# Edge sums of a graph attention kernel: score parts accumulated on TensorE, a logit as a maximum of two sums, and the clamp at zero behind the exponential

## What is computed

```python
def gnn_ref(xn, src, dst, W, att_src, att_dst):
    xp = xn @ W                          # layer 1: by head, 8 x 32
    a_src, a_dst = xp @ att_src, xp @ att_dst
    e = leaky_relu(a_src[src] + a_dst[dst], 0.2)
    emax = segment_max(e, dst)           # a bound serves as well
    ex = exp(e - emax[dst])
    denom = segment_sum(ex, dst)
    return segment_sum(ex[:, None] * xp[src], dst) / denom
```

## Time and profile before

| | |
|---|---|
| runs | 1872.51, 1877.23, 1879.56 us; median 1877.23 |
| the profiled execution's own time | 1874.21 us, span 1872.5 us |
| PE, busy share of the span | 1518.0 us, 81% |
| DVE | 1154.5 us, 62% |
| ACT | 658.4 us, 35% |
| POOL | 1009.8 us, 54% |
| mean granted TensorE clock | 0.924 |

### The profile page before, as it was taken

The page is one execution under the profiler, slowest core; times in us unless marked ns, Lnnn a source line. Parts: engine busy times, 40 slices in busy tenths (PEclk is TensorE's granted clock), DMA queues, the critical chain, the costliest instruction groups (busy, mean ns, idle before and its releaser), DMA issues. The chain is left out here.

```text
span 1872.5 us, 33346 instructions
## 1 busy us (share of the span) xinstructions
PE 1518.0 (81%) x9468; PEld 1261.2 (67%) x9468; DVE 1154.5 (62%) x3311; ACT 658.4 (35%) x2160; POOL 1009.8 (54%) x1093
## 2 busy tenths in 40 slices
PE   5488888898898968999845887878888867899990
PEld 4355656687775657999823776766666656799990
DVE  7586767775686662222174988878888888412214
ACT  4432222234334653333234334533233236432320
POOL 3577776777771003555404777777777721255540
PEclk9699999899999989999968999999999985999995
DMA  6533333344340056676563444444444304677657
GB/s 143 145 106 106 107 104 83 106 107 108 106 107 25 1 190 199 208 214 211 151 164 95 108 110 109 109 109 109 109 109 109 107 5 138 187 214 213 212 165 208
DMA packets 147994, 244.17 MB, mean 130 GB/s; under 512 B 53370, under 2 KB 83369, under 8 KB 147559
## 3 DMA queue, kind: packets, MB, share of 16 engines
q0 software_dynamic: 48384, 134.19, 26.0%
q1 hardware_dynamic: 97306, 106.27, 19.4%
q10 hardware_dynamic: 2124, 1.54, 0.4%
HBM read 210.48 MB, written 31.21 MB: 129 GB/s over the span
## 5 line engine op out<-in xcount | busy, mean ns | idle before, releaser
L683 POOL DMA_INDIRECT es_rows<-table,eall x784 | 746.1, 952 | 336.6 <-issue 235.0
L703 PE MATMUL bank<-es_msg,es_one 128*125 128x264 f32 x976 | 255.1, 406 | 88.9 <-DVE es_msg L826 88.8
L703 PE MATMUL bank<-es_rows,es_won 128*125 x976 | 262.5, 415 | 70.2 <-DVE es_won L823 69.7
L766 ACT ACTIVATE es_oneT<-bank 125x512 bf16<-125x512 f32 x244 | 145.3, 596 | 365.2 <-PE bank L722 364.8
L703 PEld LDWEIGHTS bank<-es_msg,es_one 128*125 128x125 f32 x976 | 177.2, 191 | 126.1 <-DVE es_msg L826 98.3
L703 PEld LDWEIGHTS bank<-es_rows,es_won 128*125 128x125 f32 x976 | 185.6, 200 | 104.2 <-issue 76.6
L1400 DVE TENSOR_TENSOR xT<-bank,xT 128x256 f32<-128x256 f32 x112 | 47.5, 424 | 327.1 <-PE bank L1251 327.1
L1294 ACT ACTIVATE xT<-bank,ffn_b1s 128x128 f32<-128x128 f32 x448 | 128.1, 369 | 299.9 <-PE bank L1241 299.9
L1241 PE MATMUL bank<-ffn_xbT,ffn_w 128*128 128x128 f32 x1792 | 219.6, 276 | 0.0
L1251 PE MATMUL bank<-ffn_w,xT 128*128 x896 | 211.6, 379 | 0.0
L1241 PEld LDWEIGHTS bank<-ffn_xbT,ffn_w 128*128 128x128 f32 x1792 | 210.4, 193 | 0.1
(11 more groups left out here) (447 smaller groups left out, 2338.7 us busy)
## 6 DMA issues: line engine op xcount, KB each, us to landing
ffn_w<-in_L_ffn_W SPq DMA_DIRECT2D x112, 512.0 KB
es_rows<-table,eall POOLq DMA_INDIRECT x784
ffn_w<-yrows SPq DMA_DIRECT2D x20, 560.0 KB
ffn_w<-in_L_ffn_W SPq DMA_DIRECT2D x2, 4096.0 KB
xrows<-acc SPq DMA_DIRECT2D x10, 560.0 KB
table<-acc SPq DMA_DIRECT2D x5, 577.5 KB
table<-acc SPq DMA_DIRECT2D x5, 564.4 KB
out_x<-xs SPq DMA_DIRECT2D x5, 560.0 KB
```

What stands on the lines that cost most here:

```text
L683: pool.indirect_dma_start(rows[:, q % R, w, :], None, m.table[H], bass.IndirectOffsetOnAxis(ap=m.eall[:, at:at + 1], axis=0)).then_inc(gat ...
L703: ins = pe.matmul(sum_banks[p % 2][0:P, 0:W], left, right, start=(w == 0), stop=(w == BW - 1))
L766: a.activation(oneT[:, p % 2, :], turn_bank[0:P, :], ACT.Copy).then_inc(kept, 1)
```

## The change

It moves work from the edge to the node and from DVE to PE, and reorders DVE's queue. The maximum is written as `max(s + (a - m), 0.2 s + (0.2 a - m))`. The two values `a - m` and `0.2 a - m` are prepared per node, ahead of the loop, with two more operations. The three bf16 parts are no longer side by side but are added by PE in PSUM: twelve score matmuls of 2H columns instead of four of 6H. The reduce and the buffer `near` go. Two operations read the scores from PSUM, and a third takes the maximum. The clamp goes from the z group: the weighing takes `min(weight, 1)` within its one instruction (it becomes a scalar_tensor_tensor), and with eight heads ACT makes the second exponential from a Relu. The wait for `ready` and two of the z group's operations now stand ahead of the mark. The scores of step p wait for these two of step p - 1.

```diff
                 def scores(p):
                     pe.wait_ge(kept, p + 1)
                     if p >= 1:
-                        pe.wait_ge(zchain, 4 * p - 3)
+                        pe.wait_ge(branched, 2 * p)
                     for w in range(BW):
-                        ins = pe.matmul(scores_of[p % 2][:, w, :], oneT[:, p % 2, w * 128:(w + 1) * 128],
-                                        stage[:, p % 4, :], start=True, stop=True)
+                        for c in range(3):
+                            ins = pe.matmul(scores_of[p % 2][:, w, :], oneT[:, p % 2, w * 128:(w + 1) * 128],
+                                            stage[:, p % 4, c * 2 * H:(c + 1) * 2 * H], start=(c == 0), stop=(c == 2))
                     ins.then_inc(scored, 1)
...
                         a.activation(wts[:, p % 2, :, :], z[:, p % 2, :, :], ACT.Exp).then_inc(exped, 1)
+                        a.activation(below[:, p % 2, :, :], z[:, p % 2, :, :], ACT.Relu, scale=-1.0).then_inc(bounded, 1)
                         if p >= 2:
                             a.wait_ge(summed, p - 1)
-                        a.activation(msg[:, p % 2, :, D:D + H], z[:, p % 2, :, :], ACT.Exp).then_inc(laid, 1)
+                        a.wait_ge(bounded, p + 1)
+                        a.activation(msg[:, p % 2, :, D:D + H], below[:, p % 2, :, :], ACT.Exp, scale=-1.0).then_inc(laid, 1)
...
-                k.link(v.tensor_copy(piece[0], whole))
-                k.link(v.tensor_tensor(rest[:, :, :], whole, piece[0], ALU.subtract))
+                k.link(v.tensor_tensor(whole[:, :, 0:H], reach, top, ALU.subtract))
+                k.link(v.scalar_tensor_tensor(whole[:, :, H:2 * H], reach, SLOPE, top, ALU.mult, ALU.subtract))
+                k.link(v.tensor_copy(piece[0], whole[:, :, :]))
+                k.link(v.tensor_tensor(rest[:, :, :], whole[:, :, :], piece[0], ALU.subtract))
...
-                        v.tensor_tensor(won[:, p % 2, :, :], one[:, p % O, :, :], wts[:, p % 2, :, :].to_broadcast([128, BW, P]),
-                                        ALU.mult).then_inc(weighed, 1)
+                        v.scalar_tensor_tensor(won[:, p % 2, :, :], wts[:, p % 2, :, :].to_broadcast([128, BW, P]), 1.0,
+                                               one[:, p % O, :, :], ALU.min, ALU.mult).then_inc(weighed, 1)
...
                     if valid(p3):
+                        here = rows_of(p3, D, D + H)
+                        v.wait_ge(ready, p3 + 1)
                         v.wait_ge(scored, p3 + 1)
-                        v.tensor_reduce(near[:, p3 % 2, :, :], scores_of[p3 % 2].rearrange("p w (c x) -> p w x c", c=3),
-                                        AX.X, ALU.add).then_inc(zchain, 1)
+                        if H > 1 and p3 >= 2:
+                            v.wait_ge(laid, p3 - 1)
+                        v.tensor_tensor(zq, here, scores_of[p3 % 2][:, :, 0:H], ALU.add).then_inc(branched, 1)
+                        v.scalar_tensor_tensor(yq, here, SLOPE, scores_of[p3 % 2][:, :, H:2 * H], ALU.mult, ALU.add).then_inc(branched, 1)
                     if valid(p):
                         mark(p)
                     if valid(p3):
-                        here = rows_of(p3, D, D + H)
-                        v.wait_ge(ready, p3 + 1)
-                        v.wait_ge(zchain, 4 * p3 + 1)
-                        if H > 1 and p3 >= 2:
-                            v.wait_ge(laid, p3 - 1)
-                        v.tensor_tensor(zq, here, near[:, p3 % 2, :, 0:H], ALU.add).then_inc(zchain, 1)
-                        v.wait_ge(zchain, 4 * p3 + 2)
-                        v.scalar_tensor_tensor(yq, zq, SLOPE, zq, ALU.mult, ALU.max).then_inc(zchain, 1)
-                        v.wait_ge(zchain, 4 * p3 + 3)
-                        v.tensor_tensor(zq, yq, near[:, p3 % 2, :, H:2 * H], ALU.subtract).then_inc(zchain, 1)
-                        v.wait_ge(zchain, 4 * p3 + 4)
-                        v.tensor_scalar(zq, zq, 0.0, None, ALU.min).then_inc(zed, 1)
+                        v.wait_ge(branched, 2 * p3 + 2)
+                        v.tensor_tensor(zq, zq, yq, ALU.max).then_inc(zed, 1)
```

More of the change, by code:

```diff
@@ L613, in edge_sums @@
         stage = sb("_stage", [P, 4, 3 * 2 * H], BF16)
-        near = sb("_near", [128, 2, BW, 2 * H])
         if H == 1:
@@ L621, in edge_sums @@
         early = (won if H == 1 else msg)[0:P, :, :, :].rearrange("p a w x -> p (a w x)")
-        rest = early[:, 0:NT * 2 * H].rearrange("p (t x) -> p t x", t=NT)
+        rest, whole = [early[:, i * NT * 2 * H:(i + 1) * NT * 2 * H].rearrange("p (t x) -> p t x", t=NT) for i in range(2)]
         z = sb("_z", [128, 2, BW, H])
         y = sb("_y", [128, 2, BW, H])
+        below = sb("_below", [128, 2, BW, H])
         gathered = [sem(f"_gathered{r}") for r in range(R)]
-        landed, freed, split, split_chain, marked, turned, kept, scored, zchain, zed, exped, weighed, summed, added = [
-            sem(n) for n in ("_landed", "_freed", "_split", "_split_chain", "_marked", "_turned", "_kept", "_scored", "_zchain", "_zed",
-                             "_exped", "_weighed", "_summed", "_added")]
+        landed, freed, split, split_chain, marked, turned, kept, scored, branched, zed, exped, bounded, weighed, summed, added = [
+            sem(n) for n in ("_landed", "_freed", "_split", "_split_chain", "_marked", "_turned", "_kept", "_scored", "_branched", "_zed",
+                             "_exped", "_bounded", "_weighed", "_summed", "_added")]
         ends_set, laid, ready = sem("_ends_set"), sem("_laid"), sem("_ready")
@@ L640, in edge_sums @@
         wts = m.bank[6][:, NBLK * BW:NBLK * BW + 2 * BW * H].rearrange("p (s w h) -> p s w h", s=2, w=BW)
-        scores_of = [m.bank[1][:, i * BW * 6 * H:(i + 1) * BW * 6 * H].rearrange("p (w x) -> p w x", w=BW) for i in (0, 1)]
+        scores_of = [m.bank[1][:, i * BW * 2 * H:(i + 1) * BW * 2 * H].rearrange("p (w x) -> p w x", w=BW) for i in (0, 1)]
         def valid(p):
@@ L788, in _ @@
                     v.tensor_tensor(self_z[:, :, :], self_z[:, :, :], m.adm[:, :, 1:2], ALU.subtract).then_inc(self_zed, 1)
-                whole = m.adm[:, :, 0:2 * H]
+                reach, top = m.adm[:, :, 0:H], m.adm[:, :, H:2 * H]
                 piece = [parts[:, :, i * 2 * H:(i + 1) * 2 * H] for i in range(3)]
@@ L822, in weigh @@
                             v.wait_ge(summed, p - 1)
-                        v.tensor_tensor(won[:, p % 2, :, :], one[:, p % O, :, :], wts[:, p % 2, :, :].to_broadcast([128, BW, P]),
-                                        ALU.mult).then_inc(weighed, 1)
-                    else:
-                        v.tensor_tensor(msg[:, p % 2, :, 0:D].rearrange("p w (h x) -> p w h x", h=H),
-                                        rows_of(p, 0, D).rearrange("p w (h x) -> p w h x", h=H),
-                                        wts[:, p % 2, :, :].unsqueeze(3).to_broadcast([128, BW, H, D // H]),
-                                        ALU.mult).then_inc(weighed, 1)
+                        v.scalar_tensor_tensor(won[:, p % 2, :, :], wts[:, p % 2, :, :].to_broadcast([128, BW, P]), 1.0,
+                                               one[:, p % O, :, :], ALU.min, ALU.mult).then_inc(weighed, 1)
+                    else:
+                        v.scalar_tensor_tensor(msg[:, p % 2, :, 0:D].rearrange("p w (h x) -> p w h x", h=H),
+                                               wts[:, p % 2, :, :].unsqueeze(3).to_broadcast([128, BW, H, D // H]), 1.0,
+                                               rows_of(p, 0, D).rearrange("p w (h x) -> p w h x", h=H),
+                                               ALU.min, ALU.mult).then_inc(weighed, 1)
                 for i in range(STEPS + 5):
```

## The result

The changed kernel takes **1889.14 us** (median of 20 runs, 1881.63 to 1902.51); the kernel before took 1874.44 in the 20 runs beside them (1867.54 to 1880.32). The ratio is 1.0085, with a 95% interval of 1.007 to 1.010: 0.85% slower, 14.7 us. The forecast was 1898 us: +20.7 on the 1877.23 us that the first three runs of the kernel before gave. The profiled execution took 1892.33 us with a span of 1890.5, 18.0 us more than the span before, so the trace shown is of a run somewhat above the median.

The account below looks back on a forecast made before the run. The prediction saw the first stage paced by PE and its handover with DVE, with gathers near as the next limit. Terms of +19.2 us (first stage) and +1.5 (second) gave +20.7 on 1877.23: 1898 us, range 1864 to 1928.

Parts of the forecast that it names:

- Scores on PE: Eight more score matmuls add 0.20 us per iteration on PE's path: +13.2 us first stage, +4.8 second.
- The z group behind a wait: DVE's steps after waiting for ready: z to add grows to 1.00 us, costing +8.4 us first stage, +2.9 second.
- Without a wait: First-stage iterations where DVE is never idle: reduce to add falls from 1.45 to 1.00 us, 13 times, -5.9 us.
- The new wait of PE: PE's next scores wait for both sums, which wait for ready; late every eighth iteration, 15 x 0.2 = +3.0 us.
- Weighing and ScalarE: The weighing's new form with the clamp, and ScalarE's Relu plus second Exp in the second stage, cost nothing.
- A weighing at half rate: Rival: the weighing's new form runs at half rate, mainly in the second stage; about 1950 us, chance 0.04.
- Second stage outside the pairs: Second-stage steps before about 1290 us and after 1500: DVE's savings bring 1.4 us just before the pairs, 4.8 together after.
- the pair: Two iterations of the second stage's loop through PE and DVE, predicted at about 9.07 us instead of 8.75.
- The ring's waits of POOL: Gathers' waits for a free slot among eight blocks, 14.8 us before, predicted to grow by some 15 us.
- DVE sets the pace: Rival: DVE's total work limits both stages, so six operations instead of eight make it faster; 1850 us, chance 0.15.
- the matmuls fall into PE's waits: Rival: the added score matmuls hide in PE's waits for the weighing, leaving +2.7 us; 1880 us, chance 0.15.
- Adding in place: Rival: score matmuls adding into the same columns stall PE at 182 ns each; +113, 2011 us, chance 0.04.

Follow-up runs that it names:

- experiment 8: The changed kernel with the mark ahead of the wait for ready and its twelve score matmuls issued twice (24): 1895.78 us, ratio 1.0119.
- experiment 1: The kernel before, with each score matmul issued three times into the same place, nothing else changed: 1891.43 us, ratio 1.009.
- experiment 3: The changed kernel with the mark put back ahead of the wait for ready, twelve score matmuls kept: 1860.46 us, ratio 0.9917.
- experiment 4: The changed kernel with mark ahead of the wait for ready, four wide matmuls and reduce restored, scores waiting for the reduce: 1858.71 us, ratio 0.991.
- experiment 6: The changed kernel with the mark ahead of the wait for ready and only one of three score parts (four matmuls): 1854.40 us, ratio 0.9882.
- experiment 2: The changed kernel with only the first of the three score parts, so four score matmuls instead of twelve: 1874.72 us, ratio 0.9995.
- experiment 7: Experiment 4 with the add also moved ahead of the wait for ready: 1858.87 us, ratio 0.9913.
- experiment 5: The kernel before, with only the mark moved, to behind the second of the z group's four operations: 1937.68 us, ratio 1.0334.

## Why the prediction was right, and where it was not

The forecast had the sign, the main cost and the time within 9 us. That its sum came within 6 us of the measured difference is in part luck: it had +19.2 in the first stage and +1.5 in the second, and the traces show +8.2 and +4.6.

**Scores on PE, +18.0 us (13.2 and 4.8).** Right. Measured by adding them alone: 16.7 us, of which 7.1 and 6.1 in the stages of the profiled run. By taking them away from the change: 14.4 us, with 11.6 and 5.9 in the stages. The price for each iteration is the predicted one (0.30 - 0.11 = 0.19 us), and adding into the same columns doesn't stall. What failed is the count of 66 iterations for every surrounding: 7.1 us are 36 of them, 11.6 are 58, and 25.2 in experiment 8 are 84. The path is not a fixed list. Up to step 40 of the first stage experiment 1 had lost 0.3 us, all the rest came later. The clock may be a part too: in the first stage it was 0.91 before and 0.93 with the added matmuls (the stretch of the earlier trace rows, in experiment 1 and the change alike). The groups of sums there that are over a fifth longer than their median (first start to last start) lie 18.3 us beyond it before and 15.8 in experiment 1. That is 2.5 of the 6.1 us that are missing, if all of it lies on the path.

**The z group behind a wait, +8.4 and +2.9.** This is the term that was most mis-sized. I took 0.58 from the mark to the maximum and 0.20 from there to the add, 1.00 us in all. Measured: 0.87 (median) in the first stage and 0.90 in the second, +0.09 and +0.02: the add starts 0.07 to 0.10 behind the maximum. That it doesn't wait for the maximum can't be the whole reason. It didn't wait for the clamp before either, and started 0.19 behind it (median, both stages). In experiments 3, 4, 6 and 8 the maximum follows at once on the sum that it waits for, and the add again starts 0.19 behind it. In the change and in experiment 2 the mark lies between sum and maximum. The add has register work of its own (its ISA row in DVE's order). My reading is that this work is done during the mark here, and costs its 0.1 us where the operation ahead of it is itself held by a wait. It fits that in experiment 7, first stage, a side operation starts 0.08 behind such a held maximum; no run isolates it. An iteration of the first stage, changed kernel:

```profile
424.86 0.16 DVE L845 TENSOR_TENSOR es_z<-es_rows,bank 128x4 f32<-128x4 f32 x1 [1.43 <-ACTq L781]
...
425.65 0.16 DVE L851 TENSOR_TENSOR es_z<-es_z,es_y 128x4 f32<-128x4 f32 x1
425.72 0.42 DVE L814 TENSOR_TENSOR acc<-acc,bank 125x258 f32 x1
```

By my own counts that is 38 x 0.09 + 24 x 0.02 = +3.9 instead of +11.3, a difference of 7.4 us, a little more than the whole miss of 6.0 (20.7 against 14.7 by the medians). The other terms missed too, and their misses largely cancel.

**Without a wait, -5.9.** Its sign holds: experiment 2, which has the z group and no added matmuls, has a first stage 3.4 us shorter than before, where my terms without the scores made it 6.0 longer (8.4 - 5.9 + 3.0 + 0.5). With the measured z group it is 3.4 - 5.9 + 0.5 = -2.0, which leaves nothing for the next. No run isolates the 5.9 itself.

**The new wait of PE, +3.0.** The wait came (18.4 us over 24 times), and no cost of it shows: it is 22.3 and 26.1 us in the kernels at 1860 and 1854 us, and 20.3 in the one that equals the kernel before. I take it to fall into time in which PE would have waited for the weighing anyway (its waits for that fell by 12.5 us in the first stage); no run isolates it.

**Weighing and ScalarE, nothing.** Right: 672 and 1222 ns against 669 and 1218, and experiment 2 leaves no room for more. The second stage's weighing waited 5.1 us in all for ScalarE's exponential, and 0.5 before. A weighing at half rate, my rival of some 35 us or more, did not come. The Trainium skill (Vector Engine (DVE) Microarchitecture Reference, Points that are easy to get wrong) states that rate for the form with two sources in SBUF that are not bf16. The weighing has one operand in PSUM, so its rows don't test the rule; the 418 ns of the earlier trace rows, with both in SBUF, speak against it.

**Second stage outside the pairs, -6.2.** Partly. The pairs from step 72 to 112 gave +4.4 us, and the tail gave back 2.8, not 4.8. Some 2.4 us were lost between steps 64 and 72, where one group of sums took 3.65 us, with a granted clock of 0.50 (its lower level, 1.2 GHz) from 1321.9 to 1325.3 us and of 1.00 on both sides. The trace of experiment 2, which has the same order of DVE's queue, shows the same group at 3.08 us and these steps 1.4 us longer than before, and no other trace shows this group slow, so it may belong to the order and not to one execution. The stage as a whole gave +4.6 where +1.5 was expected, and the first gave +8.2 where +19.2 was.

**The signs.** The score group, its 0.30 us and the weighings came as named. z to add was to be 1.0 us and is 0.87 and 0.90; the pair was to be 9.07 and is 8.97. The ring's waits of POOL were to grow by some 15 us and grew by 1.1: the loss of the first stage lies behind its last gather. The wait for ready in a pair was to be about 0.7 longer and is 1.8 longer at the place shown (3.05 against 1.27), and DVE's busy time fell by 142 us over the span (1154.5 to 1012.5), not by about 100.

**The rivals.** That DVE sets the pace is refuted: it is busy 157 us less in the two stretches and the kernel is slower. The Trainium skill (VectorE: DVE Perf Modes, Rules for kernel authors) advises to lower the number of operations and to consider restructuring a tensor_reduce on a hot path. Here the trade brought nothing. With the mark ahead in both, the kernel with the reduce on DVE (experiment 4, 1858.71 us) equals the one with the parts added on PE (experiment 3, 1860.46); without either, experiment 6 is 4.3 us below experiment 4. The reduce stands ahead of the wait for ready. That the matmuls fall into PE's waits is refuted by experiment 1. Adding in place doesn't stall.

**What I did not see,** and what the experiments gave: the change holds a gain and a loss of about the same size. Two sums side by side and the clamp off the path cut z to add from 0.88 to about 0.5 us (experiments 3, 4). That is worth 16 us; the gathers, which the first stage meets, cap it. The mark in the middle takes the same 0.4 us back (experiment 2, at the time of the kernel before). Without the shortened group, the mark at that place costs 62 us. The best version with all of the computation is experiment 4, **1858.71 us**, 1.6% under the changed kernel and 0.9% under the kernel before; experiments 3 and 7 are as good within 2 us.

## What to carry to other kernels

An operation's place in its queue can matter more than its length. Ahead of the wait that paces the loop, a reduce of 0.27 us (start to start, eight heads) cost 4 us of 1859 at most, and a mark of 0.58 us stood there in every fast kernel; behind it, the mark alone took back all that a shorter chain had won. So when you shorten a chain behind a wait, don't fill the freed gap with work that could stand ahead of the wait.

Moving work from an idle engine to the one on the path is a loss even when the busy shares look balanced: price the moved work by starts on the path (25 ns a small matmul, times the iterations that pass through it; that count moved from 36 to 84 here), and test it by adding that work alone.

Ask early how far the next limit is. Here it was 12 us away in the first stage of the kernel before (507.3 against 495.5, its gathers), and four of the five versions with the mark ahead met it (the fifth, with 24 matmuls, is held by PE); in the second stage two waits for ScalarE came next, one of them for a row of another branch. That these two are its limit was not tested.

## What the runs showed that was not expected

- A wait may cost twice. In experiment 5 the longer waits of PE for the weighing (2.00 us ahead of the sums shown) went with a fall of the granted clock from 1.00 to 0.90 in 1400 to 1500 us, and sums of 2.04 us that took 3.42.
- Runs of one kernel spread along its clock. Over 20 runs of the changed kernel the time falls with the mean granted clock: 1881.6 and 1882.5 us at 0.930, 1902.5 us at 0.919 (correlation -0.96; which of the two drives the other it doesn't tell). Between kernels it can be the other way round: with more matmuls the clock was higher, 0.927 and 0.933 in the traces of experiments 1 and 8 against 0.924 before, and both kernels are slower.
- Small matmuls that add into the same columns three in a row start 25 ns apart (median in both stages of the change), the same as ones that don't (experiment 1).
- Two small operations of DVE of which the second doesn't need the first start 0.08 us apart on 4 elements and 0.10 on 32 (the two sums of the changed kernel, medians); ones that wait for each other 0.19 to 0.23. An operation with register work of its own behind one that waited starts 0.19 behind it, needed or not.
